# The feed-forward work of one token chunk cut into small pieces and placed in quarter slots of the next chunk's attention, with part of it on GpSimd

## What is computed

```
x = x + xcond0(layernorm(x), ctx)     # 16 heads of 16: softmax(scale*(q k^T * tau + delta)) v, then Wo
x = x + ffn0(layernorm(x))            # router over 8 experts, top 1, x @ expert_w of that expert, times its weight
x = x + xcond1(ctx, layernorm(x))     # local attention: a window around p_t; mask, softmax, times a
                                      # Gaussian of the distance, tanh([context, x] W_c^T)
x = x + ffn1(layernorm(x))            # h = gelu(..), logits over 64 slots, top 8 softmax = alpha; slots
                                      # = alpha^T x; a GRU, attention and layer norm on 64 slots; alpha @ slots
```

## Time and profile before

| what | value |
|---|---|
| three runs | 1251.07 us median (1246.15 to 1251.75) |
| profiled execution, its own time | 1245.92 us |
| its span, first to last instruction | 1244.2 us |
| mean granted TensorE clock | 0.885 |
| busy: PE, DVE, ACT, POOL | 1050.7, 813.3, 549.0, 44.1 us |

### The profile page before, as it was taken

The page is one execution under the profiler, slowest core; times in us unless marked ns, Lnnn a source line. Parts: engine busy times, 40 slices in busy tenths (PEclk is TensorE's granted clock), DMA queues, the critical chain, the costliest instruction groups (busy, mean ns, idle before and its releaser), DMA issues.

```text
span 1244.2 us, 13613 instructions
## 1 busy us (share of the span) xinstructions
PE 1050.7 (84%) x4796; PEld 419.7 (34%) x4796; DVE 813.3 (65%) x1814; ACT 549.0 (44%) x1020; POOL 44.1 (4%) x54
## 2 busy tenths in 40 slices
PE   6457999999989988889899889898998898786556
PEld 3332232223333334323333243233332342243424
DVE  4447987788776676577777765677777666544242
ACT  4121267676644345456444454575444455400210
POOL 3110000000000000000000000000000000000000
PEclk9776699999999998799999987899999898987665
DMA  8995000000100000001000000010000000100421
GB/s 242 148 115 196 1 2 13 14 13 1 31 13 1 11 3 1 14 1 48 13 2 1 14 1 13 1 48 1 14 1 14 1 13 1 47 1 0 120 68 67
DMA packets 44238, 40.65 MB, mean 33 GB/s; under 512 B 10109, under 2 KB 42334, under 8 KB 43914
## 3 DMA queue, kind: packets, MB, share of 16 engines
q1 hardware_dynamic: 41594, 38.17, 13.0%
q10 hardware_dynamic: 2496, 1.35, 0.7%
q0 software_dynamic: 80, 0.26, 0.2%
HBM read 29.52 MB, written 10.59 MB: 32 GB/s over the span
## 4 chain that ended last, share of the span: by engine, by line
PE 62%; issue 18%; DVE 13%; ACT 2%; DVEq 2%; POOL 1%; DMA 1%; POOLq 1%; SPq 0%; ACTq 0%
PE ps_o L772 18%; PE ps_e L934 15%; PE ps_m L698 13%; PE ps_m L803 7%; DVE mx L1082 6%; PE ps_m L997 1%; ACT probs L589 1%; DVE xb L1145 1%; PE ps_m L887 1%; PE ps_m L828 1%; PE ps_m L868 1%; PE ps_m L889 1%; DVE bst L1065 1%; PE ps_m L789 1%; DVE xn L1074 1%
## 5 line engine op out<-in xcount | busy, mean ns | idle before, releaser
L1082 DVE TENSOR_REDUCE mx<-ps_m 128x1 f32<-128x401 f32 x1102 | 569.2, 568 | 221.2 <-PE ps_m L698 218.6
L589 ACT ACTIVATE probs<-ps_e 128x512 f32<-128x512 f32 (+1 forms) x832 | 454.9, 595 | 449.8 <-PE ps_e L934 447.5
L698 PE MATMUL ps_m<-k_stack,q_stack 99*128 99x401 bf16 x1102 | 378.9, 362 | 64.0 <-DVE mx L1082 63.8
L934 PE MATMUL ps_e<-q_stack,k_stack 101*128 101x512 bf16 (+1 forms) x832 | 335.8, 404 | 5.9 <-ACT probs L589 3.1
L772 PE MATMUL ps_o<-probs,v_heads 128*32 128x512 f32 (+1 forms) x1664 | 238.8, 648 | 0.0
L934 PEld LDWEIGHTS ps_e<-q_stack,k_stack 101*128 101x128 bf16 (+1 forms) x832 | 84.5, 102 | 301.0 <-ACT probs L589 193.2
L698 PEld LDWEIGHTS ps_m<-k_stack,q_stack 99*128 99x128 bf16 x1102 | 111.7, 101 | 190.3 <-DVE mx L1082 129.1
L803 PE MATMUL ps_m<-expert_w,xnT 128*128 128x512 f32 x256 | 131.8, 615 | 10.5 <-DVE xb L1145 5.9
L1145 DVE SCALAR_TENSOR_TENSOR xb<-ps_m,hot,xb 128x256 f32<-128x256 f32 x112 | 54.2, 484 | 17.4 <-PE ps_m L803 8.1
L803 PEld LDWEIGHTS ps_m<-expert_w,xnT 128*128 128x128 f32 x256 | 47.6, 197 | 52.0 <-issue 29.1
L772 PEld LDWEIGHTS ps_o<-probs,v_heads 128*32 128x32 f32 (+1 forms) x1664 | 33.8, 111 | 69.2 <-issue 64.9
(11 more groups left out here) (213 smaller groups left out, 615.2 us busy)
## 6 DMA issues: line engine op xcount, KB each, us to landing
q_stack<-q_parts SPq DMA_DIRECT2D x114, 64.0 KB, 2.3
k_stack<-k_parts SPq DMA_DIRECT2D x18, 256.0 KB, 14.1
q_parts<-attn_chunk SPq DMA_DIRECT2D x6, 384.0 KB, 5.4
expert_w<-in_expert_wT SPq DMA_DIRECT2D x2, 1024.0 KB, 5.9
xres<-in_x SPq DMA_DIRECT2D x4, 512.0 KB, 3.8
x<-xres SPq DMA_DIRECT2D x4, 512.0 KB, 3.1
probs<-x SPq DMA_DIRECT2D x1, 2048.0 KB, 9.9
out<-probs SPq DMA_DIRECT2D x4, 512.0 KB, 2.9
```

What stands on the lines that cost most here:

```text
L589: act.activation(probs[0:n, k % 2, h, :], ps_e[h % 2][0:n, :], ACT.Exp).then_inc(s["exp_done"], 1)
L698: pe.matmul(ps_m[:, (UNITS * n1 + u) % RING, 0:SPLIT], qst[0:MAX_ROW, g, h, P * t:P * t + P], kst[0:MAX_ROW, HG * g + h, QUARTER_START[q]: ...
L934: pe.matmul(ps_e[h % 2][0:n, :], kst[0:ROWS, HG * g + h, P * st:P * st + n], qst[0:ROWS, g, h, :], start=True, stop=True).then_inc(s["qk_r ...
L1082: dve.tensor_reduce(mx[:, q, col:col + 1], ps_m[:, (UNITS * n1 + u) % RING, 0:SPLIT], AX.X, ALU.max)\
```

## The change

**One list of jobs.** JOBS names, for each job, the job that it follows, a distance in quarter slots (one quarter is one head's part of a slot, so 208 in a chunk), and for how long it holds its bank. `places()` turns it into AT, the quarter of each job: ota 10, y0 15, y1 17, t1a 28, router 33, e0 38, then one expert every 4 quarters or so to e15 at 106, gb0 112, t2a 125, score0 130, aTa 145, z0 150, z1 158, t3a 178, h 183, logits 189, slots 203, alphaT 207.

**Pieces.** `behind(c)` of each engine is now a generator that yields the quarter in which its next piece is due, and `go_on` runs the pieces up to the present quarter. On PE a piece is one or two transposes or the matmuls of one or half an output tile; on DVE, statistics come two tiles at a time, the small chains of the router and of the logits two or three instructions at a time. The max units of a slot are fixed to quarters (1, 2, 1, 1).

**GpSimd.** In the chunks that run behind another one, GpSimd does the three normalisations (`normal`, 4 instructions of 128x256 each), the softmax scaling of the local attention (4 of 128x256), and the sum of the third block (2 of 128x512). Behind the last chunk, alone, DVE still does them.

**Folded factors.** The window mask is multiplied once into `win_k` and the Gaussian once into the window's context rows, at the start, instead of into the scores and probabilities of each chunk.

```
-BEHIND = {3: ["ota", "otb"], 5: ["y0"], 6: ["y1"], 9: ["t1a", "t1b"], 10: ["router"],
-          **{11 + i: [f"e{i}"] for i in range(8)}, 15: ["gateT", "e4"], 19: ["gb0", "gb1"],
-          **{20 + i: [f"e{8 + i}"] for i in range(8)}, 30: ["t2a", "t2b"], 31: ["score0", "score1"], 34: ["aTa", "aTb"],
-          35: ["z0"], 36: ["z1"], 39: ["t3a", "t3b"], 40: ["h"], 41: ["logits"], 44: ["slots", "alphaT"]}
...
+def units_at(k, h):
+
+    units = units_of(k)
+    return units[:1] if h == 0 else units[1:1 + len(units) - 3] if h == 1 else units[len(units) - 4 + h:len(units) - 3 + h]
...
+JOBS = [("ota", None, 10, 3), ("otb", "ota", 2, 3), ("y0", "otb", 3, 3), ("y1", "y0", 2, 3), ("t1a", "y1", 11, 3),
+        ("t1b", "t1a", 2, 3), ("router", "t1b", 3, 2), ("e0", "router", 5, 6)]
+JOBS += [(f"e{i}", f"e{i - 1}", 4, 6) for i in range(1, 4)] + [("gateT", "e3", 3, 3), ("e4", "gateT", 1, 6)]
+JOBS += [(f"e{i}", f"e{i - 1}", 4, 6) for i in range(5, NE)]
+JOBS += [("gb0", f"e{NE - 1}", 4, 4), ("gb1", "gb0", 2, 4), ("t2a", "gb1", 11, 3), ("t2b", "t2a", 2, 3),
+         ("score0", "t2b", 3, 3), ("score1", "score0", 2, 3), ("aTa", "score1", 13, 3), ("aTb", "aTa", 2, 3),
+         ("z0", "aTb", 3, 9), ("z1", "z0", 8, 9), ("t3a", "z1", 20, 3), ("t3b", "t3a", 2, 3), ("h", "t3b", 3, 5),
+         ("logits", "h", 6, 2), ("slots", "logits", 14, 6), ("alphaT", "slots", 4, 3)]
...
+def places():
+
+    fixed = sorted([(q, q + 3) for q in O_AT] + [(q, q + 2) for q in M_AT])
+    ring, at = [(0, 0), (0, 0)], {}
+    for name, after, lag, hold in JOBS:
+        q = at[after] + lag if after else lag
+        while True:
+            while fixed and fixed[0][0] < q:
+                ring.append(fixed.pop(0))
+            q = max(q, ring[-2][1])
+            if not fixed or fixed[0][0] >= q and ring[-1][1] <= fixed[0][0]:
+                break
+            q = max(q, fixed[0][0] + 1)
+        at[name] = q
+        ring.append((q, q + hold))
+    return at
...
+def go_on(work, quarter):
+
+    while work and work[1] <= quarter:
+        work[1] = next(work[0], NEVER)
...
+            def normal(src, job, c):
+
+                pool.drain()
+                wait_filled(pool, job, c)
+                for t in range(TT):
+                    last = pool.tensor_scalar(xn[:, t, 0:D], src[:, t, :], mv[:, t, 0:1], rstd[:, t:t + 1],
+                                              ALU.subtract, ALU.mult)
+                last.then_inc(s["xn_ready"], 1)
...
+                rsqrt(NC + 3 * c + 2)
+                if not last:
+                    normal(xb, "t1b", c)
+                    pool.wait_ge(s["recip_ready"], c + 1)
+                    for t in range(TT):
+                        a = pool.tensor_scalar(work[:, t, :], work2[:, t, :], st4[:, 6, t:t + 1], None, ALU.mult)
+                    a.then_inc(s["a_ready"], 1)
+                    for i in range(2):
+                        wait_taken(pool, f"z{i}", c)
+                        x3 = pool.tensor_tensor(xres[:, 2 * i:2 * i + 2, :], xb[:, 2 * i:2 * i + 2, :],
+                                                work[:, 2 * i:2 * i + 2, :], ALU.add)
+                    x3.then_inc(s["x3_ready"], 1)
+                rsqrt(NC + 3 * c + 3)
+                if not last:
+                    normal(xres, "t2b", c)
...
+                yield AT["t1a"] + 2
+                take_xnT(0, "t1a", c)
+                yield AT["t1b"] + 2
+                take_xnT(1, "t1b", c)
...
+            def turned(name, c, src, k):
+
+                bank_free(pe, name, c)
+                for t in range(TT):
+                    if t == 2:
+                        yield AT[name] + 1
+                    mm = pe.transpose(bank(name, c)[:, P * t:P * t + P], src[:, t, P * k:P * k + P], ident[:])
+                filled(mm, name, c)
+
+            def rows_by(name, c, tiles, rows, weights):
+
+                bank_free(pe, name, c)
+                for i, t in enumerate(tiles):
+                    if i:
+                        yield AT[name] + i
+                    for k in range(KT):
+                        mm = pe.matmul(bank(name, c)[:, D * i:D * i + D], rows[:, k, P * t:P * t + P], weights[:, k, :],
+                                       start=(k == 0), stop=(k == KT - 1))
+                filled(mm, name, c)
...
-                            pe.matmul(o, aT[:, kk, tok:tok + P], win_v[:, kk, :], start=(kk == 0), stop=False)
-                        for kk in range(KT):
-                            mm = pe.matmul(o, xnT[:, kk, tok:tok + P], wc[:, KT + kk, :], start=False, stop=(kk == KT - 1))
+                        for k in range(KT):
+                            yield AT[name] + 4 * t + k
+                            pe.matmul(o, aT[:, k, tok:tok + P], win_v[:, k, :], start=(k == 0), stop=False)
+                        for k in range(KT):
+                            yield AT[name] + 4 * t + 2 + k
+                            mm = pe.matmul(o, xnT[:, k, tok:tok + P], wc[:, KT + k, :], start=False, stop=(k == KT - 1))
                     filled(mm, name, c)
...
                     if st == 0:
                         pe.wait_ge(m_loaded[g], 32 * (c + 1))
-                    units = iter([(c, j, u) for j, u in units_of(k)])
-                    spare = len(units_of(k)) - HG
                     for h in range(HG):
-                        if h == 2:
-                            if not first:
-                                behind(c - 1, k - SHIFT, units)
-                            if first or not has_expert(k - SHIFT):
-                                for _ in range(spare):
-                                    next_unit(units)
                         need(pe, s["exp_done"], HG * SLOTS * c + HG * k + h - 1)
                         pe.matmul(ps_e[h % 2][0:n, :], kst[0:ROWS, HG * g + h, P * st:P * st + n],
                                   qst[0:ROWS, g, h, :], start=True, stop=True).then_inc(s["qk_ready"], 1)
-                        next_unit(units)
-                    assert next(units, None) is None
-                    if k or not first:
+                        for j, u in units_at(k, h):
+                            max_unit(u, c, j)
+                        go_on(work, HG * k + h)
+                        if HG * k + h in M_AT:
+                            max_rows(NG * c + max_end(k - 1))
+                        if HG * k + h in O_AT and (g or c):
+                            turn_o(NG * c + g - 1)
+                    if k or c:
                         pv(c, k - 1)
-                    if st == 2 and (g or not first):
-                        turn_o(NG * c + g - 1)
-                    if max_end(k - 1) is not None:
...
+                if kind == "W":
+                    dve.wait_ge(s["win_psum"], 1)
+                    dve.tensor_tensor(win_k[:], ps_x[:].rearrange("p (k w) -> p k w", k=KT),
+                                      keep[:].unsqueeze(1).broadcast_to((P, KT, W)), ALU.mult).then_inc(s["win_masked"], 1)
+                    dve.wait_ge(s["gauss_ready"], 1)
+                    dve.tensor_tensor(enc_win[:], enc_win[:], gauss[:].unsqueeze(1).broadcast_to((P, KT, W)), ALU.mult)\
+                       .then_inc(s["win_scaled"], 1)
...
+            def spread_stats(src, at):
+
+                dve.drain()
+                for t in range(TT):
+                    if t % 2 == 0:
+                        yield at + t // 2
+                    dve.bn_stats(bst[:, t, :], src[:, t, :])
+                yield at + 2
+                dve.drain()
+                for t in range(TT):
+                    last = dve.bn_aggr(mv[:, t, :], bst[:, t, :])
+                last.then_inc(s["var_ready"], 1)
...
+
+                for i in range(2):
+                    yield AT[f"score{i}"] + 2
+                    at = slice(2 * i, 2 * i + 2)
+                    take_sum(work[:, at, :], neg_mask[:].unsqueeze(1).broadcast_to((P, 2, W)), f"score{i}", c)
+                    yield AT[f"score{i}"] + 3
                     dve.drain()
```

696 lines of the change are left out of this document (345 added, 351 removed).

## The result

The changed kernel takes 1237.25 us in the median of four runs (1234.71 to 1237.76), the kernel before 1251.26 in the runs beside it: a ratio of 0.9898, 95% interval 0.9876 to 0.9921. It is 1.0% faster, where 6.9% were forecast. The profiled execution has a span of 1235.1 us and a mean granted clock of 0.899.

The account below looks back on a forecast made before the run. PE close to full, plus waits and a slow clock. Per chunk 168 + (54 - 12.6) + 10 + 6 = 225 us against 252.9, three times 27.5 less, 82 us: 1164, predicted as 1165 us; range 1118 to 1208.

Parts of the forecast that it names:

- excess idle: waits for `xn`: PE before the transposes of `xn`: 1 us of wait at t2a (bounds 0 and 1.9), none at t1a and t3a.
- excess idle: all other: PE's remaining idle per chunk: 4 us at maxima and experts, 4 for ACT's copies, 1 for gelu before the logits.
- (b): GpSimd in the normalisation's path: one `xn` instruction 0.5 us, four 2.0, chain 3.5; PE waits 1 us, bounds 0 and 1.9.
- rival D: GpSimd's `xn` and scaling much slower: gain used up at 9.7 us for four; at 3 us each 1273 us; chance 0.05.
- rival C: Waits move to ACT's copies, GpSimd's chain and DVE's small pieces: 239 us a chunk, 1205 us, range 1190 to 1239; chance 0.16.
- Clock: PE at half clock behind idle stretches: with less idle, in shorter pieces, 6 us lost per chunk instead of 18; bounds 0 and 16.
- DVE's lumps: Statistics split 2 + 2 + aggregates, with work leaving DVE: PE's excess idle at maxima and experts from 18 us to 4, bounds 2 and 12.
- Hidden work: PE's pieces spread over about 45 slots instead of 30, 0.28 us hidden in each: 12.6 us instead of 8.4 per chunk.
- ACT's copies: PE waits 0.8 us for ACT at y0, router, score0, z0 and h: 4 us per chunk, bounds 0 and 5; largest new releaser.
- start and tail: Program start and the work behind chunk 3, alone with normalisation on DVE: 0 change, tail bounds -4 and +3 us.
- expert slots: Slots with expert work, 4.6 us before: the prediction would be wrong if they got longer, DVE and PE being near full there.
- collisions: DVE and GpSimd working together: taken as 0 us; 10.4 us of DVE time if every new GpSimd instruction held DVE for its length.

Follow-up runs that it names:

- The dose: Changed kernel with six instead of four `xn` instructions per normalisation on GpSimd (two tiles done twice, with drains): 1261.17 us, ratio 1.0126.
- the distance: Changed kernel with t1a and t2a 15 quarters behind their predecessors instead of 11, t3a 23 instead of 20, slots 12 instead of 14: 1208.78 us, ratio 0.9679.
- the first experiment: Changed kernel with only the three normalisations (`xn`) of a chunk back on DVE, two tiles per quarter: 1195.66 us, ratio 0.9582.

## Why the prediction was wrong

The forecast of 225 us a chunk met 251.7 (mean of three). By its own terms, per chunk:

| term | forecast | measured |
|---|---|---|
| attention alone (chunk 0) | 168 | 167.6 |
| PE's work behind, of it hidden | 54, 12.6 | 54, 5 |
| excess idle: waits for `xn` | 1 | 9.4 |
| excess idle: all other | 9 | 14 (before: 22) |
| loss at half clock | 6 | 11.4 |
| sum | 225 | 252 |

Excess idle is over the 3.5 us of chunk 0; the loss is half of the 20.5, 23.9 and 23.9 us at half clock; 5 is what is left, not a measurement. The prediction took 18 us of excess idle time in the kernel before, from the maxima and the experts alone; with all groups of chunk 2 it is 25.2 - 3.5 = 22.

**The step that failed is (b), one `xn` instruction on GpSimd at 0.5 us, bounds 0.24 and 0.7.** It takes 1.22 us, and the scaling, the form with one operation, 0.93. The bounds came from a cast and a sum with whole tiles as operands, and I took rates per element from them. Neither carries a scalar for each partition, and the bound from above was no bound. The other half of the step was the time that the list leaves: 5.1 us at t1a by counting quarters, 3.3 measured, since DVE makes the aggregates later than their quarter. Both halves count: with only one of them right the wait of 3.2 us would have been put at 1.4 (6.5 - 5.1) or 0.2 (3.5 - 3.3). The dose (six instructions, +8 us a chunk), the distance (-28 us) and the undoing (-41.6) show it three ways. It is rival D's mechanism at half of D's price, four `xn` at 4.9 us where D decides from 9.7. D's own formula gives 4 x 4.9 - 11.4 = 8.2 us of waits a chunk for it, and 9.4 were measured. That is close in part by luck: place by place it gives 1.3, 3.8 and 1.1 us for the 3.2, 3.6 and 2.6 measured at t1a, t2a and t3a, and 2.0 at the scaling, where PE waits for 0.6. But it would have shown the size, and I had tried it at its far end alone, as if nothing lay between 0.7 and 2.4 us for one instruction.

The time of 1237 us lies at the far end of rival C (1190 to 1239), which names GpSimd's chain among the waits that move and has 12 us of clock, 11.4 measured. It has no price for `xn`, though, and 18 us of excess idle time where 23.5 were measured; its hidden work of 13 us was not there either.

The failed step does not account for the whole miss. With `xn` back on DVE the kernel takes 1196 us, still 31 above the 1165 forecast, though inside the range. There the idle time over that of chunk 0 is 15 us a chunk in place of 10, the clock is as forecast, and some 3 us of PE's work are hidden in place of 12.6.

**Clock.** The idle time "in shorter pieces" and its 6 us of loss failed with it: the waits are 2.6 to 3.6 us long, longer than that of the earlier trace rows, and 17 of chunk 2's 24 us at half clock begin at their ends. Without these waits, in the first experiment, the loss is 5.1 us in the mean of the chunks, near the forecast.

**DVE's lumps.** The maxima's waits did fall from 18 to 6 us, forecast 4. But the reason given, the statistics cut in halves, isn't the reason: with large pieces on DVE they rise to 10 only, and with the statistics alone in one piece to 7.8 at most. And I had left out that smaller pieces free a bank later. The waits before the experts, in the 18 us with 3.0, should have gone too; they rose to 5.1, and that is as much as the 5 us by which "all other" idle time is above its forecast.

**Hidden work.** 12.6 us in place of 8.4 didn't come. The same account, with the loss as half of the half-clock stretches, leaves 5 us in the changed kernel and 9 in the kernel before (168 + 54 + 22.5 + 18.2 - 253.3, with the idle and half-clock time as means of its chunks), so by this account less is hidden, not more. That small pieces of PE are better than large ones is still right: large pieces cost 14 to 24 us in the same list. Why the gain against before doesn't show isn't settled.

**ACT's copies** were forecast at 0.8 us each. PE's idle time before y0, router, score0, z0 and h is 0.45, 0.53, 0.48, 0.41 and 0.65 us: 2.5 for 4. Only z0's is put down to ACT in the trace. They are not the largest new releaser; `xn` is.

**Right:** chunk 0 unchanged; start and tail nearly (the start is 1.1 us longer, the tail 5.1 shorter, just outside its bound of 4); expert slots that got no longer (median 4.56 us before and after); the scaling without a wait that matters (0.6 us of PE); and no collisions: six maxima take 2.95 us, 0.49 each, while GpSimd is at work beside them, as in the earlier trace rows. The rule of the Trainium skill ("SBUF — State Buffer", Who interferes with whom) that a reduction never takes the lock is borne out by these rows. The advice of the Trainium skill in "GPSIMD Engine Reference", Engine selection, to keep elementwise work on VectorE is borne out too. Its remark there that work with one input runs at about line rate is not: with one tensor input and scalars per partition the row is 1.22 us, three times the 0.41 of DVE.

## What to carry to other kernels

An instruction that is moved to another engine has to be priced on that engine in its own form; where no row shows it, the range has to reach up to the time at which the moved work decides, and every value below that has to be tried too; here the wait began long before it. What the receiving engine does must then be set against the measured time between its input and the in-order engine that waits for it, since a wait on TensorE can cost more than its length. Here the three waits, 9.4 us a chunk, cost 13.9, about half of it as half clock; when they were made 7.8 us longer, that cost 8.2.

When a change consists of several parts that each have a reason, undo them one at a time: here the list (with ACT's places, the fixed max units and the folded factors, which weren't separated) and PE's small pieces carried all the gain, the three normalisations on GpSimd took most of it back, and DVE's small pieces were worth nothing or less.

## What was not expected of the hardware

A `tensor_scalar` with two scalars per partition takes 1.22 us for 128x256 on GpSimd and 0.41 on DVE, and one with one scalar 0.93 us. A `tensor_tensor` of twice the elements, 128x512, takes only 1.30 us on GpSimd: the form with two scalars takes nearly twice as long per column of 128 elements as the one with two tensors (4.8 against 2.5 ns).

Useless matmuls in a wait can pay: twelve of 128x128 before each of three waits a chunk took some 20 us off the kernel, with the granted clock in the chunk at 0.99 instead of 0.95.
